# Attention of a fused transformer step: two key tiles folded into one 128-wide softmax, and the rotary step on one engine

## The reference

```python
q = rope((x @ wq).reshape(B, S, 32, 128)); k = rope((x @ wk).reshape(B, S, 8, 128))
v = (x @ wv).reshape(B, S, 8, 128)
scores = einsum('bqhgd,bshd->bhgqs', q.reshape(B, S, 8, 4, 128), k) * 128 ** -0.5
allowed = (j <= i) & (j > i - 128)          # i: query, j: key
attn = softmax(where(allowed, scores, finfo.min), axis=-1)
out = einsum('bhgqs,bshd->bqhgd', attn, v).reshape(B, S, 4096) @ wo
```

## Time and profile before

| | |
|---|---|
| median of 3 runs | 954.69 us (953.87 to 955.3) |
| the profiled execution | 955.38 us, span 953.3 us |
| TensorE busy | 916.7 us, 96% |
| VectorE busy | 602.9 us, 63% |
| GpSimd busy | 521.6 us, 55% |
| ScalarE busy | 482.2 us, 51% |
| mean granted TensorE clock | 0.993 of full speed |
| DMA | 61.37 MB, 64 GB/s over the span |

### The profile page before, as it was taken

The page is one execution under the profiler, slowest core; times in us unless marked ns, Lnnn a source line. Parts: engine busy times, 40 slices in busy tenths (PEclk is TensorE's granted clock), DMA queues, the critical chain, the costliest instruction groups (busy, mean ns, idle before and its releaser), DMA issues. The chain is left out here.

```text
span 953.3 us, 15404 instructions
## 1 busy us (share of the span) xinstructions
PE 916.7 (96%) x4576; PEld 765.6 (80%) x4576; DVE 602.9 (63%) x1492; ACT 482.2 (51%) x1097; POOL 521.6 (55%) x401
## 2 busy tenths in 40 slices
PE   5799999999999999999999999999998999999996
PEld 4578888888888888888888888888786788888885
DVE  7666666666566665666566566656774666657556
ACT  4456655656665656566566556655543232222213
POOL 4557656654765666466566646555214454435436
PEclk9989999999999999999999999999999999999999
DMA  7011010100111010011102000101214655365452
GB/s 239 5 41 61 18 34 23 45 26 19 44 33 33 22 44 22 22 44 33 33 0 66 22 22 26 29 0 34 68 34 126 173 165 147 101 181 157 119 176 88
DMA packets 84300, 61.37 MB, mean 64 GB/s; under 512 B 3632, under 2 KB 71472, under 8 KB 84272
## 3 DMA queue, kind: packets, MB, share of 16 engines
q1 hardware_dynamic: 83552, 59.91, 21.5%
q10 hardware_dynamic: 720, 1.11, 0.3%
HBM read 58.92 MB, written 2.10 MB: 64 GB/s over the span
## 5 line engine op out<-in xcount | busy, mean ns | idle before, releaser
L51 PE MATMUL ps<-xt_hi,w_lo 128*128 128x512 f32 x608 | 239.1, 393 | 5.7 <-ACT sil L283 1.8
L52 PE MATMUL ps<-xt_lo,w_hi 128*128 128x512 f32 x608 | 238.4, 392 | 0.0
L53 PE MATMUL ps<-xt_hi,w_hi 128*128 128x512 f32 x608 | 238.0, 392 | 0.0
L693 ACT ACTIVATE probs<-probs,neg_max 128x256 f32<-128x256 f32 (+1 forms) x256 | 120.2, 471 | 86.2 <-DVE neg_max L924 86.2
L801 POOL TENSOR_TENSOR work<-work,sin 128x512 f32<-128x512 f32 x80 | 104.3, 1304 | 100.7 <-ACT work L675 100.5
L51 PEld LDWEIGHTS ps<-xt_hi,w_lo 128*128 128x128 f32 x608 | 115.0, 189 | 30.8 <-issue 4.3
L53 PEld LDWEIGHTS ps<-xt_hi,w_hi 128*128 128x128 f32 x608 | 114.7, 189 | 24.6
L52 PEld LDWEIGHTS ps<-xt_lo,w_hi 128*128 128x128 f32 x608 | 114.9, 189 | 22.5
L939 DVE TENSOR_TENSOR pt_lo<-ps,pt_hi 128x512 fp32r<-128x512 f32 (+1 forms) x64 | 69.7, 1089 | 75.7 <-ACT pt_hi L699 75.7
L933 DVE TENSOR_SCALAR probs<-probs,inv 128x256 f32<-128x256 f32 (+1 forms) x256 | 114.1, 508 | 2.3
L809 POOL TENSOR_TENSOR work<-work 128x512 f32<-128x512 f32 x75 | 97.1, 1294 | 25.4 <-DVE work L913 17.6
(11 more groups left out here) (82 smaller groups left out, 1761.9 us busy)
## 6 DMA issues: line engine op xcount, KB each, us to landing
work<-L_attn_wq SPq DMA_DIRECT2D x32, 256.0 KB, 2.7
work<-L_attn_wo SPq DMA_DIRECT2D x32, 256.0 KB, 2.6
work<-L_ffn_gate_w SPq DMA_DIRECT2D x14, 256.0 KB, 4.2
work<-L_ffn_gate_z SPq DMA_DIRECT2D x14, 256.0 KB, 4.8
work<-L_ffn_gate_s SPq DMA_DIRECT2D x14, 256.0 KB, 5.4
work<-L_ffn_up_w SPq DMA_DIRECT2D x14, 256.0 KB, 3.5
work<-L_ffn_up_z SPq DMA_DIRECT2D x14, 256.0 KB, 4.1
work<-L_ffn_up_s SPq DMA_DIRECT2D x14, 256.0 KB, 4.6
```

Source lines behind the costliest of these rows:

```text
L51: pe.matmul(out, stat[1], mov[0], start=first, stop=False)
L52: pe.matmul(out, stat[0], mov[1], start=False, stop=False)
L53: return pe.matmul(out, stat[0], mov[0], start=False, stop=last)
L693: act.activation(probs[:, h, cols], probs[:, h, cols], ACT.Exp, scale=-1.0, bias=neg_max[:, h:h + 1], accum_out=total[:, h:h + 1]).then_in ...
```

## The change

Scores. `scores` writes two key tiles per head as before (one at j = 0, where the zero padding is gone). VectorE then folds: where the causal mask says that a key of the own tile is in the future, `copy_predicated` puts the score of the tile before in its place, in PSUM; at j = 0 the mask is added. One `tensor_reduce` gives the four negated maxima. ScalarE takes the exponentials of 128 columns straight from PSUM and, after VectorE's reciprocal, scales them as well. `turn_probs` has 4 transposes per tile, into one bank. VectorE unfolds: it multiplies the turned probabilities by a 0/1 mask for each key tile, into `kept`. ScalarE makes the high part from that, one operation for each key tile, and GpSimd the low part, which VectorE made before.

Rotary step. All four operations are VectorE's, in place: two multiplies by sin that read one half of the partitions and write the other, the bank times cos back into the bank, and the sum into `roped`. The scale of the scores goes into the tables (each times 128 ** -0.25). `swap` and `direct` are gone.

Order. There are three projection banks. Projections 1, 3, 5 come ahead of `project_out` in tiles 0 to 2, projections 2 and 4 behind `weigh_values` in tiles 0 and 1, and projection 0 of the unit after next stands in tile 3. The FFN pieces and products of the last unit come one tile earlier, and SP's wait for `rope_split` is gone (VectorE's `dequantise` waits for it instead). In the prologue VectorE normalises the second half of x ahead of the rotations. The tables are four loads in place of three.

```diff
@@ softmax and projections, PSUM layout
-        ps_proj = ps[:, 0:2, :]
-        ps_score = ps[:, 2:4, :].rearrange("p a (h c) -> p (a h) c", h=2)
-        ps_pt = ps[:, 4:6, :]
+        ps_proj = ps[:, 0:3, :]
+        ps_pt = ps[:, 3, :]
+        ps_score = ps[:, 4:6, :].rearrange("p a (h w c) -> p (a h) w c", h=2, w=2)
...
-        SPLIT_AT = {(0, 1): (0, 1), (0, 2): (2, 3), (0, 3): (4, 5), (1, 0): (6,), (1, 1): (7,), (1, 2): (8,), (1, 3): (9,)}
-        FFN_AT = ((-2,), (-1,), (0,), (1,))
-        bank = lambda b, k: ps_proj[:, (PROJ * b + k) % 2, :]
+        SPLIT_AT = {(0, 0): (0,), (0, 1): (1,), (0, 2): (2,), (0, 3): (3, 4), (1, 0): (5,), (1, 1): (6,),
+                    (1, 2): (7, 8), (1, 3): (9,)}
+        FFN_AT = {(0, 3): (-2,), (1, 0): (-1,), (1, 1): (0,), (1, 2): (1,)}
+        BEFORE, AFTER = (1, 3, 5), (2, 4, None)
+        BANK = ((0, 1, 2, 0, 1, 2, 0), (1, 2, 0, 1, 2, 0, 1))
+        FREE = ((-1, 0, -2), (-2, -1, 0))
+        bank = lambda b, k: ps_proj[:, BANK[b][k], :]
...
+        def windows(j):
+            return range(0 if j else 1, 2)
...
             sp.wait_ge(w_split, NKV * NPIECE)
             for at in range(-2, EARLY):
-                if at == -1:
-                    sp.wait_ge(rope_split, UNITS * 5)
                 fw.load(sp, 0, at, *fw.piece(at), 0)
@@ TensorE
-                wait(pe, proj_drained, unit * PROJ + (k - 1))
+                wait(pe, proj_drained, unit * PROJ + (k - 2 if k >= 3 else FREE[b][k]))
...
             def scores(n, unit, b, j, heads=range(GQ)):
-                wait(pe, shifted, n * GQ)
+                wait(pe, exp_done, n * GQ)
+                w0 = windows(j)[0]
                 for h in heads:
                     wait(pe, rope_split, unit * 5 + (h + 2))
                     q = [t[:, b, h, j * P:(j + 1) * P] for t in (q_hi, q_lo)]
-                    k = [t[:, b, j * P:(j + 2) * P] for t in (k_hi, k_lo)]
-                    last = three_passes(pe, ps_score[:, h, :], q, k, True, True)
-                    if h % 2:
+                    k = [t[:, b, (j - 1 + w0) * P:(j + 1) * P] for t in (k_hi, k_lo)]
+                    last = three_passes(pe, ps_score[:, h, w0:2, :].rearrange("p w c -> p (w c)"), q, k, True, True)
+                    if h == GQ - 1:
                         last.then_inc(scores_ready, 1)
...
-                    for w in range(0 if j else 1, 2):
-                        last = pe.transpose(ps_pt[:, w, h * P:(h + 1) * P], probs[:, h, w * P:(w + 1) * P], ident[:, :])
+                    last = pe.transpose(ps_pt[:, h * P:(h + 1) * P], probs[:, h, :], ident[:, :])
...
+                        turn_probs(n)
+                        if ahead and j == QB - 1:
+                            turn_v(un, bn)
                         if j < QB - 1:
-                            scores(g * 8 + (4 * b + j + 1), unit, b, j + 1)
-                        ahead_project(*((1,), (2,), (4, 5), (6,))[j])
-                        if not ahead and j == 3:
-                            ffn_product(1, GATE)
+                            scores(n + 1, unit, b, j + 1)
+                        elif ahead:
+                            scores(n + 1, un, bn, 0)
+                        if ahead and j < QB - 1:
+                            project(gn, un, bn, BEFORE[j])
+                        elif not last:
+                            project(g + 1, unit + 2, b, 0)
+                        elif not ahead and j < QB - 1:
+                            ffn_product(*((0, GATE), (0, UP), (1, GATE))[j])
                         project_out(g, b, j)
...
+                        if not ahead and j == QB - 1:
+                            ffn_product(1, UP)
                         weigh_values(n, unit, b, j)
...
+                        if ahead and j < QB - 1 and AFTER[j]:
+                            project(gn, un, bn, AFTER[j])
@@ ScalarE
-            def exps(n, j):
-                cols = slice(0 if j else P, 2 * P)
+            def exps(n):
+                act.wait_ge(max_done, n + 1)
                 for h in range(GQ):
-                    act.wait_ge(shifted, n * GQ + (h + 1))
-                    act.activation(probs[:, h, cols], probs[:, h, cols], ACT.Exp, scale=-1.0, bias=neg_max[:, h:h + 1],
+                    act.activation(probs[:, h, :], ps_score[:, h, 1, :], ACT.Exp, bias=neg_max[:, h:h + 1],
                                    accum_out=total[:, h:h + 1]).then_inc(exp_done, 1)
...
+            def normalise(n):
+                act.wait_ge(inv_done, n + 1)
+                for h in range(GQ):
+                    act.activation(probs[:, h, :], probs[:, h, :], ACT.Copy, scale=inv[:, h:h + 1]).then_inc(probs_ready, 1)
+
+            def hi_of_probs(unit, j):
+                for i, w in enumerate(windows(j)):
+                    act.wait_ge(kept_done, parts(unit, j) + (i + 1))
+                    act.activation(pt_hi[:, w, :], kept[:, w, :], ACT.Copy).then_inc(pt_hi_done, 1)
@@ GpSimd
+            def lo_of_probs(unit, j):
+                for i, w in enumerate(windows(j)):
+                    pool.wait_ge(pt_hi_done, parts(unit, j) + (i + 1))
+                    pool.tensor_tensor(pt_lo[:, w, :], kept[:, w, :], pt_hi[:, w, :].bitcast(F32),
+                                       ALU.subtract).then_inc(pt_split, 1)
@@ VectorE
+            def rope(unit, b, i):
+                par, half, at = (5 * b + i) % 2, P // 2, bank(b, i)
+                dve.wait_ge(proj_ready, unit * PROJ + (i + 1))
+                wait(dve, rope_split, unit * 5 + (i - 1))
+                dve.tensor_tensor(roped[0:half, par, :], at[half:P, :], sin[half:P, :], ALU.mult).then_inc(sin_done, 1)
+                dve.tensor_tensor(roped[half:P, par, :], at[0:half, :], sin[0:half, :], ALU.mult).then_inc(sin_done, 1)
+                dve.wait_ge(sin_done, unit * 10 + (2 * i + 2))
+                dve.tensor_tensor(at, at, cos[:, :], ALU.mult).then_inc(cos_done, 1)
+                dve.wait_ge(cos_done, unit * 5 + (i + 1))
+                dve.tensor_tensor(roped[:, par, :], at, roped[:, par, :], ALU.add).then_inc(proj_drained, 1)
+
+            def fold_and_max(n, j):
+                dve.wait_ge(scores_ready, n + 1)
+                dve.memset(waited[:, :], 0.0)
+                own = ps_score[:, :, 1, :]
+                over_h = lambda m: m.unsqueeze(1).broadcast_to([P, GQ, P])
+                if j:
+                    dve.copy_predicated(own, over_h(causal[:, :]).bitcast(I32), ps_score[:, :, 0, :]).then_inc(folded, 1)
+                else:
+                    dve.tensor_tensor(own, own, over_h(causal[:, :]), ALU.add).then_inc(folded, 1)
+                dve.wait_ge(folded, n + 1)
+                dve.tensor_reduce(neg_max[:, :], own, mybir.AxisListType.X, ALU.max, negate=True).then_inc(max_done, 1)
...
+            def unfold(n, unit, j):
+                dve.wait_ge(pt_ready, n + 1)
+                for w in windows(j):
+                    dve.tensor_tensor(kept[:, w, :].rearrange("p (h c) -> p h c", h=GQ),
+                                      ps_pt.rearrange("p (h c) -> p h c", h=GQ),
+                                      keep[:, w, :].unsqueeze(1).broadcast_to([P, GQ, P]), ALU.mult).then_inc(kept_done, 1)
...
+                        unfold(n, unit, j)
+                        if more:
+                            fold_and_max(n + 1, (j + 1) % QB)
+                        if ahead and 0 < j < QB - 1:
+                            rope(un, bn, AFTER[j - 1])
+                        if ahead and j == QB - 1:
                             lo_of_v(un, bn)
...
+                        if more:
+                            invert(n + 1)
+                        if ahead and j < 2:
+                            rope(un, bn, BEFORE[j])
                         if ahead and j == 2:
                             drain_v(un, bn)
-                        if j < QB - 1:
-                            add_y(g, b, j)
+                        if not last and j == QB - 1:
+                            rope(unit + 2, b, 0)
...
+                        add_y(g, b, j)
                         lo_of_o(n, j)
```

304 lines of the change are left out of this document (99 added, 205 removed).

## The result

The changed kernel takes 920.33 us (median of four runs, 919.74 to 920.50) where the kernel before takes 954.59 us beside it (953.87 to 955.30): a ratio of 0.964 [0.9623, 0.9657], 34.3 us less. The forecast was 934.0 us with a range of 923 to 957. The sign was right.

A forecast was written before the change was run, and what follows sets the result against it. TensorE's instruction stream was taken as the bound: -24.5 (transposes) + 0 + 0 (chains) + 4.5 (prologue) - 1 (end of attention) = -21.0 us, from a median of 954.69 to about 934 us, range 923 to 957.

The forecast's parts named there:

- TensorE is the bound, and what leaves its stream counts in full: Attention loop: TensorE is busy 206.40 of 207 us, so every microsecond leaving its instruction stream shortens the kernel.
- Rival 4: Probability transposes are hidden, so folding does not free TensorE: 952 us, chance 0.03.
- Transposes, -24.5 us: Probability transposes at j = 1, 2, 3: 12 fewer per unit, 1.53 us each unit, times 16 is 24.5 us less.
- Narrow products, no change: Scores of j = 0, 128 instead of 256 moving columns: still a step of 0.12 us, nothing gained.
- Rivals 1 and 3: Scores of j = 0: 128 columns step at 0.23 us, 955 us; or at 0.065 us, 923.4 us; chance 0.2 each.
- Projections, output projections and the products with V keep their number and width. They are only reordered: TensorE's 512-column products in the loop: unchanged in cost, no term in the sum.
- The chain turn, unfold, split, V: 0 us: From probability transposes to products with V: VectorE, ScalarE and GpSimd finish in time, cover 2.8 us, nothing paid.
- the softmax chain: 0 us with about 0.7 us of room: Scores to transposes in the loop: no cost, slack about 1 us at j = 2 and 0.7 us at j = 3.
- Rival 2: VectorE's queue bounds the loop at j = 1 and 2 through slow predicated copies: up to 977 us, chance 0.1.
- 2x - 0.8 - 0.7: Loop stop per unit in us if each predicated copy on VectorE takes x longer; 2.7 us for a 2.8 us copy.
- Prologue, +4.5 us: Before the loop: first tile's last transpose at about 54.5 instead of 50.41 us, +4, taken as +4.5 for the lower clock.
- End of attention, -1 us: Last unit: FFN pieces one step earlier remove 1.3 us of idle time, one step may cost 0.5; taken as -1.

## Why the prediction was right in sign and short in size

Point by point, by the steps of the forecast.

- **TensorE is the bound, and what leaves its stream counts in full**: right. The loop has 340.00 busy us in 340, and every change of the unit appears in the total. Rival 4 is out.
- **Transposes, -24.5 us**: right. The runs give 1.50 us per unit, 24.0 in all.
- **Narrow products, no change**: a small miss. The step is 0.111 us where I kept 0.120: 0.13 us per unit, 2 us. The argument from the weight load (0.107) was nearer than the value I took, though one of its premises is wrong: in `three_passes` the second and the third product (L52, L53) have the same weights. They are loaded again each time all the same (4576 loads for 4576 products). Rivals 1 and 3, with a chance of 0.2 each, were both wrong, and they alone set the range's ends.
- **"Projections, output projections and the products with V keep their number and width. They are only reordered"**: this is the sentence that failed, twice over. It costed at nothing two things that the trace before could have shown. First, has an output projection at 0.23 us (308.35, 308.58), and I took one step for all products of 512 columns. Over the loop the output projections step at 0.231 to 0.237 and the projections beside them at 0.227, and the change moves the allocations (the diff as printed above leaves these lines out): 0.40 us per unit in the old stream, 6.4 us in 16 units (5.7 measured as a whole). Second, the stop ahead of the output projections of j = 3, 0.45 us per unit or 7 us: I looked at the waits of the transposes alone, and took "issue" for no wait. Together these are the 1.0 us by which each unit beats the forecast, with the narrow products' 0.13.
- **The chain turn, unfold, split, V: 0 us, and the softmax chain: 0 us with about 0.7 us of room**: right. One more reduction leaves the unit unchanged within 0.1 us, a second one does not. One price in the chain was too low: a scaling on ScalarE takes 390 ns, not the 0.31 us worked out, 0.3 us more for four. The prices, from the groups of VectorE and ScalarE of the changed kernel:

```profile
L876 DVE COPY_PREDICATED ps<-causal_sb,ps 128x512 f32<-128x512 int32 x48 | 33.2, 691 | 5.9 <-issue 1.8
L865 DVE TENSOR_TENSOR ps<-ps,cos 128x512 f32<-128x512 f32 x80 | 56.0, 700 | 2.8
L675 ACT ACTIVATE probs<-probs,inv 128x128 f32<-128x128 f32 x256 | 81.6, 390 | 17.1 <-DVE inv L884 17.1
```

  The predicated copy from PSUM into PSUM takes 691 ns where 0.69 us was taken, and writing the rotation's product back into PSUM 700 ns. Both unknowns lay at the value of their width.
- **Rival 2, VectorE's queue as the bound**: did not occur at 0.69 us. Its formula (2x - 0.8 - 0.7) was too low beyond the threshold: at x = 1.38 it gives 1.3 us per unit, the stops measured 1.7, and the lower clock, for which it had no term, added 0.9. The point of decision was judged well, the slope badly: x = 0.69 us costs nothing in the unit, 1.38 us costs 42 us in all.
- **Prologue, +4.5 us**: the queue was right (rotations in VectorE's queue ahead of the first fold), its size a little high. The first scores after the first transposes start at 53.80, where they started at 50.54: +3.3, not +4. The extra 0.5 for the clock did not come: it is at its lower level for 6.8 us in both traces (48.6 to 55.4 before, 49.6 to 56.4 after), and TensorE had less work in that time after (3.6 us, 5.5 before). The means of 0.68 and 0.73 differ only by where the ten microseconds are cut.
- **End of attention, -1 us**: wrong. From unit 14 to the end the gain was 1.9 us where two units' transposes and the -1 make 4.1. I moved the FFN products earlier in my account without asking what they had stood in front of. It was once more the low part of o.
- **Sum.** In span, the forecast was -21.0 and -34.6 was measured. Of the 13.6 us between, 12.8 lie in units 1 to 13 (13 x (2.51 - 1.53)), 3.0 in prologue and unit 0 (+4.5 - 1.5 forecast, 0 measured), and -2.2 in the end. The chances have a slip of 0.01: with rival 4 faster or same, slower adds up to 0.15, not 0.16.

The range failed for the same reason: it was built from the unknown prices of operations that the diff names, and had no term for instructions that it leaves alone.

## What to carry to other kernels

An instruction that keeps its form can still change its step when a diff reorders the allocations. Compare the steps of equal products with different operands in the trace before, and where they differ, work out from sizes and order where each operand starts; here a start at a multiple of 128 bytes was worth 6 to 9 us in 920 to 955. For each product ask which short chain makes its operand and what work stands in front to cover it, and do not take idle time marked "issue" for no wait: one output projection moved ahead of the scores cost 39 us here, about 13 of them in waits for one 0.69 us operation and most of the rest in what then came late. Where a queue has less than a microsecond of room, measure the room by adding one operation, then a second.
